# Retention and balanced experts as one stage: where the routing work stands between two layers of a language-model tower

## The reference, cut to what matters

```python
# retention: 8 heads of 16, causal with decay, group norm, gate, output projection
scores = jnp.einsum('bhtd,bhsd->bhts', q, k) / jnp.sqrt(jnp.float32(dh))
out = jnp.einsum('bhts,bhsd->bhtd', scores * decay[None], v)
return jax.nn.silu(x @ W_G + _group_norm(out)) @ W_O
# balanced experts: 8 experts, each sequence by itself
t = jnp.log(jnp.clip(einsum(x, gate_weight), 1e-6))
for _ in range(8):                                  # Sinkhorn
    t = t - logsumexp(t, axis=-2, keepdims=True)    # over the 512 tokens
    t = t - logsumexp(t, axis=-1, keepdims=True)    # over the 8 experts
vals, idx = top_k(exp(t) transposed, 512 // 8)      # 64 tokens for each expert
out[idx] = vals * (x[idx] @ experts[e])             # a later expert overwrites
```

## Time and profile before

| | |
|---|---|
| median of 3 runs | 2459.11 us (2454.38 to 2466.83) |
| the profiled execution's own time | 2457.47 us |
| its span | 2455.7 us |
| busy in the span: PE, DVE, ACT, POOL | 78%, 74%, 56%, 12% |

### The profile page before, as it was taken

One profiled execution on the slowest core, in us unless ns is written; L12 is line 12 of the kernel. 1 busy time (PEld: TensorE's weight loads), 2 busy tenths in 40 slices (PEclk: granted clock), 3 DMA queues, 4 the chain that ended last, 5 costly groups with the idle time before them and its releaser, 6 DMA issues. The chain is left out here.

```text
span 2455.7 us, 33355 instructions
## 1 busy us (share of the span) xinstructions
PE 1925.8 (78%) x11810; PEld 955.2 (39%) x11810; DVE 1805.2 (74%) x5024; ACT 1383.4 (56%) x1659; POOL 285.7 (12%) x332
## 2 busy tenths in 40 slices
PE   4999995886385699999999999999999776524933
PEld 2566654665131133333333333333334432313822
DVE  2676565665698899999999999999997677641513
ACT  0232221221056999999999999999998211101400
POOL 5000111001001000000000000000000000174373
PEclk8889996885597999999999999999999888656966
DMA  6300000001000100000000000000000000314521
GB/s 191 127 1 35 1 1 20 1 1 52 0 26 29 61 1 1 1 1 1 1 1 1 1 1 1 1 1 1 1 1 1 7 0 0 147 44 126 153 68 51
DMA packets 50149, 71.20 MB, mean 29 GB/s; under 512 B 8000, under 2 KB 36176, under 8 KB 49232
## 3 DMA queue, kind: packets, MB, share of 16 engines
q1 hardware_dynamic: 41264, 46.15, 5.5%
q0 software_dynamic: 8736, 23.10, 3.2%
HBM read 39.87 MB, written 23.07 MB: 26 GB/s over the span
## 5 line engine op out<-in xcount | busy, mean ns | idle before, releaser
L1751 ACT ACTIVATE KM<-KM 128x2048 f32<-128x2048 f32 x311 | 595.5, 1936 | 3.6 <-DVE KM L1601 3.6
L1601 DVE TENSOR_SCALAR KM<-big 128x512 f32<-128x512 f32 x1244 | 513.9, 480 | 24.1 <-PE bank L1878 16.7
L1878 PE MATMUL bank<-KM,w_a_wa 128*32 128x512 f32 x2736 | 370.5, 615 | 77.3 <-ACT KM L1751 60.5
L1751 ACT ACTIVATE aa_args<-aa_args 128x2048 f32<-128x2048 f32 x153 | 294.5, 1937 | 1.5 <-DVE aa_args L1601 1.5
L184 POOL TENSOR_TENSOR nrstd<-nrstd,minus_half 128x4 f32<-128x4 f32 (+1 forms) x82 | 84.2, 1047 | 1766.2 <-DVE nrstd L161 1729.2
L1851 PE MATMUL bank<-rf_wgu,XT 128*128 128x512 f32 x512 | 280.8, 634 | 1.2 <-DVE t512b L1660 1.2
L1601 DVE TENSOR_SCALAR aa_args<-big 128x512 f32<-128x512 f32 x612 | 253.9, 481 | 6.2 <-PE bank L1878 5.9
L1878 PE MATMUL bank<-aa_args,w_a_wa 128*32 128x512 f32 x1360 | 182.7, 610 | 37.4 <-ACT aa_args L1751 28.2
L1878 PEld LDWEIGHTS bank<-KM,w_a_wa 128*32 128x32 f32 x2736 | 54.3, 108 | 287.5 <-ACT KM L1751 190.0
L1851 PEld LDWEIGHTS bank<-rf_wgu,XT 128*128 128x128 f32 x512 | 77.4, 188 | 178.0 <-issue 173.7
L1656 DVE SCALAR_TENSOR_TENSOR ST<-ST,bank 128x256 f32<-128x256 f32 x256 | 106.3, 415 | 43.9 <-ACT ST L1741 43.8
(11 more groups left out here) (387 smaller groups left out, 3279.4 us busy)
## 6 DMA issues: line engine op xcount, KB each, us to landing
queues<-zeros SPq DMA_DIRECT2D x1, 8192.0 KB, 24.8
KM<-queues SPq DMA_DIRECT2D x32, 256.0 KB, 2.9
results<-KM POOLq DMA_DIRECT2D x32, 256.0 KB, 2.8
w<-in_w SPq DMA_DIRECT2D x1, 4096.0 KB
big<-in_w_pairs SPq DMA_DIRECT2D x1, 4096.0 KB
mf_tv<-in_task_W SPq DMA_DIRECT2D x1, 2048.0 KB, 10.2
la_v<-in_task_W SPq DMA_DIRECT2D x1, 2048.0 KB, 7.7
big<-XT SPq DMA_DIRECT2D x8, 256.0 KB, 2.3
```

The costliest lines, as they stand in the source:

```text
L1601: last = nc.vector.tensor_scalar(ARG(n, step)[:, cc, :], KU[:, i * T:(i + 1) * T], q, None, ALU.add)
L1751: last = nc.scalar.activation(ARG(n, step), ARG(n, step), ACT.Tanh)
L1878: last = nc.tensor.matmul(m.bank[g][32 * cc:32 * cc + 32, :], w["a_wa"][:, 30 - 2 * k:62 - 2 * k], ARG(n, step)[:, cc, :], start=k == 0, s ...
```

## The change

The two functions become one, `retention_and_balanced_experts`, without the barrier between them and with buffers of its own for the gates and the normalised input (`xta`, so no DMA puts it aside).

1. Gate front. The norm, transposes and gate matmuls of pair 0 stand inside retention's pair 1, those of pair 1 inside pair 2, those of pairs 2 and 3 around the end of pair 3. No loops; new transposes write the banks that retention's transposes use.
2. Sinkhorn in two halves of four sequences. Half 0 has one round after each of the eight score units of retention's pair 3, and its `max` rounds follow before the variances are read. Half 1 comes after retention, with two tiles of half 0's expert sum in each of its eight rounds. The selection is done once for each half, on 32 partitions instead of 64.
3. Expert sum. DVE takes experts 0 to 3 as four chained `scalar_tensor_tensor` into `h`, two tiles alternating. ACT weighs experts 4 to 7 as before, and POOL adds those in three steps (256, 128 and 128 elements per partition), the last into `h`. Matmul results have three pairs of banks.
4. The three weights of the experts are loaded with retention's.

```diff
@@ POOL
+            nc.gpsimd.memset(SEL, 0.0).then_inc(rest_zero.sem, 1)
...
+            for n in range(HALVES * TILES):
+                pool.wait_ge(scaled.sem, scaled.at(n, 1))
+                nc.gpsimd.tensor_tensor(y[:, 0:2, :], y[:, 0:2, :], y[:, 2:4, :], ALU.add).then_inc(four_sb.sem, 1)
+                pool.wait_ge(four_sb.sem, four_sb.at(n, 1))
+                nc.gpsimd.tensor_tensor(y[:, 0, :], y[:, 0, :], y[:, 1, :], ALU.add).then_inc(two_sb.sem, 1)
+                pool.wait_ge(two_sb.sem, two_sb.at(n, 1))
+                pool.wait_ge(acc[n % 2].sem, acc[n % 2].at(n // 2, 4))
+                nc.gpsimd.tensor_tensor(h, h, y[:, 0, :], ALU.add).then_inc(out_sb.sem, 1)
@@ DVE, in the loop over retention's pairs
-                masks(i)
                 if i + 1 < PAIRS:
+                    masks(i, range(len(UNITS)))
                     norm.vector(dve, i + 1, norm.pair(i + 1), XN)
+                    if i:
+                        gate_norm(i - 1)
+                else:
+                    for u in range(len(UNITS)):
+                        masks(i, (u,))
+                        for part in range(6):
+                            balance(0, u, part)
+                    for r in range(M // 8):
+                        ranked(0, r)
...
+                if 0 < i < PAIRS - 1:
+                    gate_logits(i - 1)
...
                 if i + 1 < PAIRS:
                     states(i + 1)
+                else:
+                    gate_norm(i - 1)
@@ DVE, behind it
+            selected(0)
+            gate_norm(PAIRS - 1)
+            gate_logits(PAIRS - 2)
+            weighted(0)
+            kept(0)
+            gate_logits(PAIRS - 1)
+            for k in range(ITERS):
+                for part in range(6):
+                    balance(1, k, part)
+                    if part < 4:
+                        summed(2 * k, part)
+                        summed(2 * k + 1, part)
+            for r in range(M // 8):
+                ranked(1, r)
+            selected(1)
+            weighted(1)
+            kept(1)
+            for n in range(TILES, 2 * TILES, 2):
+                for e in range(4):
+                    summed(n, e)
+                    summed(n + 1, e)
@@ PE, the expert matmuls
+            def expert(n):
+                if n >= 3:
+                    pe.wait_ge(acc[(n - 3) % 2].sem, acc[(n - 3) % 2].at((n - 3) // 2, 4))
+                    pe.wait_ge(scaled.sem, scaled.at(n - 3, 1))
+                for q in range(2):
+                    last = nc.tensor.matmul(m.bank[E_B(n)[q]][:, :], xta[:, b * T + c * P:b * T + (c + 1) * P], w["experts"][:, 512 * q:512 * q + 512],
+                                            start=True, stop=True)
@@ PE, the order
+                    for u in range(len(UNITS)):
+                        scores(i, (u,))
+                        columns(0, u)
+                    attend(i, (0,))
+                    turn_gates(0)
+                    attend(i, (1,))
                 variances(i)
+                if nxt and i:
+                    turn_b(i - 1)
+                if nxt:
                     keys(i + 1)
                 widen(i)
+                if nxt and i:
+                    logits(i - 1)
...
+            turn_b(PAIRS - 2)
+            logits(PAIRS - 2)
+            later(0)
+            turn_b(PAIRS - 1)
+            turn_weights(0)
+            logits(PAIRS - 1)
+            expert(0)
+            expert(1)
+            for k in range(ITERS):
+                columns(1, k)
+                for n in (2 * k + 2, 2 * k + 3):
+                    if n < TILES:
+                        expert(n)
+            turn_gates(1)
+            later(1)
+            turn_weights(1)
+            pe.wait_ge(w_sb.sem, 2)
+            for n in range(TILES, 2 * TILES):
+                expert(n)
```

More of the change, by code:

```diff
@@ L897, in _, with retention_and_balanced_experts @@
             down(3)
-def retention(ctx, nc, m):
+def retention_and_balanced_experts(ctx, nc, m):
     S = range(2)
@@ L971, in states, with masks @@
                         nc.vector.tensor_tensor(ST[s][:, c * P:(c + 1) * P], TB[s][:, 0:P], w["same_head"][:, :], ALU.mult).then_inc(st_sb.sem, 1)
-            def masks(i):
-                for u, (s, half, pair) in enumerate(UNITS):
+            def masks(i, us):
+                for u in us:
+                    s, half, pair = UNITS[u]
                     dve.wait_ge(sc_ps.sem, sc_ps.at(i, u + 1))
@@ L1045, in values, with turned_b, scale @@
                     nc.scalar.copy(V[s][:, :, :], v).then_inc(v_sb.sem, 1)
+            def turned_b(i):
+                for s in S:
+                    act.wait_ge(xb_ps.sem, xb_ps.at(i, s + 1))
+                    nc.scalar.copy(xta[:, (2 * i + s) * T:(2 * i + s + 1) * T], TB[s][:, :]).then_inc(xb_sb.sem, 1)
+            def scale(n):
+                act.wait_ge(e_ps.sem, e_ps.at(n, 1))
+                if n >= 4:
+                    act.wait_ge(out_sb.sem, out_sb.at(n - 4, 1))
+                for e in range(4):
+                    last = nc.scalar.activation(YW[n % 4][:, e, :], m.bank[E_B(n)[1]][:, e * D:(e + 1) * D], ACT.Copy, scale=weight(n, 4 + e))
+                last.then_inc(scaled.sem, 1)
             act.wait_ge(wv_ps.sem, 1)
@@ L1068, in _ @@
                     values(i + 1)
+            turned_b(PAIRS - 2)
+            turned_b(PAIRS - 1)
+            for h in range(HALVES):
+                act.wait_ge(w_sb.sem, w_sb.at(h, 1))
+                for n in range(h * TILES, (h + 1) * TILES):
+                    scale(n)
         @block.tensor
@@ new lines, in logits, with columns @@
+            def logits(i):
+                if i == 0:
+                    pe.wait_ge(m.loaded["gate_w"], 16)
+                for s in S:
+                    pe.wait_ge(xb_sb.sem, xb_sb.at(i, s + 1))
+                    for c in range(NC_):
+                        t = (2 * i + s) * T + c * P
+                        last = nc.tensor.matmul(TB[s][:, c * E:(c + 1) * E], xta[:, t:t + P], w["gate_w"][:, :], start=True, stop=True)
+                    last.then_inc(lg_ps.sem, 1)
+            def columns(h, k):
+                if k == 0:
+                    pe.wait_ge(lg_sb.sem, lg_sb.at(2 * h + 1, 2))
+                    pe.wait_ge(h_sb.sem, h_sb.at(2 + h, 2))
+                else:
+                    pe.wait_ge(sink_sb.sem, sink_sb.at(h * ITERS + k - 1, 6))
+                nc.tensor.matmul(OB[0][:, 0:NC_ * HE], w["ones"][:, 0:P], G8[h][:, :], start=True, stop=True).then_inc(col_ps.sem, 1)
@@ new lines, in turn_gates, with later @@
+            def turn_gates(h):
+                pe.wait_ge(sink_sb.sem, sink_sb.at(h * ITERS + ITERS - 1, 6))
+                for c in range(NC_):
+                    last = nc.tensor.transpose(GT_B(h)[0:HE, c * P:(c + 1) * P], G8[h][:, c * HE:(c + 1) * HE], w["ident"][:, :])
+                last.then_inc(gt_ps.sem, 1)
+            def later(h):
+                if h == 0:
+                    pe.wait_ge(m.loaded["later_expert"], 16)
+                    pe.wait_ge(rest_zero.sem, 1)
+                pe.wait_ge(sel_sb.sem, sel_sb.at(h, 1))
+                nc.tensor.matmul(LATER_B(h)[0:HE, :], w["later_expert"][:, 0:HE], SEL, start=True, stop=True).then_inc(later_ps.sem, 1)
@@ new lines, in turn_weights @@
+            def turn_weights(h):
+                pe.wait_ge(w_in.sem, w_in.at(h, 1))
+                for c in range(NC_):
+                    last = nc.tensor.transpose(W_B(h)[:, c * P:(c + 1) * P], SEL[:, c * P:(c + 1) * P], w["ident"][:, :])
+                last.then_inc(w_ps.sem, 1)
+            def expert(n):
+                b, c = at_tile(n)
+                if n == 0:
+                    pe.wait_ge(m.loaded["experts"], 16)
+                    pe.wait_ge(w_sb.sem, 1)
+                if n == 2:
+                    pe.wait_ge(lg_sb.sem, lg_sb.at(PAIRS - 1, 2))
+                if n >= 3:
[4 more added lines that the diff above has]
+                                            start=True, stop=True)
+                last.then_inc(e_ps.sem, 1)
```

366 lines of the change are left out of this document (143 added, 223 removed).

## The result

| | before | changed |
|---|---|---|
| median of 15 runs each | 2459.11 us (2452.63 to 2471.04) | 2445.77 us (2439.82 to 2452.25) |
| ratio, 95% interval | | 0.9936 (0.9921 to 0.9951) |
| profiled execution, its span | 2457.47, 2455.7 us | 2440.76, 2438.5 us |
| the stage, from layer 0's last addition to layer 2's first statistics | 387.66 to 741.01 = 353.35 us | 392.90 to 723.35 = 330.45 us |

Windows of the changed kernel (columns as in the earlier trace rows): pair 1, the masks of pair 3 with the rounds of half 0, the second Sinkhorn, the last 16 tiles.

A forecast was written before the change was run, and what follows sets the result against it. PE was taken as nearly full in retention's pairs, Sinkhorn and selection as one-engine chains with the others idle. Terms 10.8 + 14.3 + 7.6 + 2.9 - 12.0 + 10.7 - 32.6 = +1.7 us gave 2461 us, range 2449 to 2475.

The forecast's parts named there:

- seven terms with a sign: Steps of the stage: +10.8, +14.3, +7.6, +2.9, -12.0, +10.7, -32.6 us; an eighth, selection of half 1, was 0.
- The second Sinkhorn: Half 1's rounds with half 0's expert sum: 5.8 us a round, 1.6 of it idle, 44.8 against 34.1: +10.7 us.
- The expert sum: The last 16 tiles after selection: 2.1 us a tile, 39.2 in all against 71.8: -32.6 us.
- PE's ring: Expert sum: PE may write tile n + 3 only after tile n is summed, stalling about 0.5 us a pair.
- Pairs 1 and 2: Retention pairs that each gain a norm, 8 transposes and 8 gate matmuls: 5.4 us each, +10.8 us.
- Masks with rounds: Pair 3's masks with half 0's Sinkhorn: a unit of 3.4 us, eight units 27.2 against 12.9: +14.3 us.
- From the last addition to the second Sinkhorn: From retention's last addition to half 1's first column sum: 22.7 us against 34.7: -12.0 us.
- (a): Rival: POOL bounds the expert sum; at 2.9 us a tile the sum is +14.5, 2474 us; chance 0.18.
- (b): Rival: PE's clock stays low in the second Sinkhorn, price +12 us, 2473 us; chance 0.08.
- (c): Rival: inserted work costs the pairs nothing, last part 1.75 us a tile, 2444 us; 0.17 with what lies beyond.
- The port: DVE and POOL disturbing each other in SBUF: 0.13 us an instruction, 2 us over the rounds, some 5 by the skill's rule.

The follow-up runs named there:

- the repeat: The changed kernel with no edit, profiled a second time on another chip: 0.9943 against the kernel before.
- the other profile of before: The kernel before with no edit, profiled a second time, one execution: stage 354.2 us, pairs 1 and 2 together 83.1 us.
- all three edits together: Changed kernel with staggered rounds, a fourth pair of banks for the last 16 tiles, and transposes behind the keys: 0.9870 against the kernel before.
- the staggered rounds: Changed kernel, second Sinkhorn only: one expert tile ahead of PE's column sum instead of two, DVE's second tile two steps later: 0.9891 against the kernel before.

## Why the prediction was wrong

The recorded forecast was no change, 2461 us in 2449 to 2475. It came out at 2445.8, below the range. The waits stand where they were put, but for two short ones, and each of the seven terms with a sign has the one it was given. The sizes were off: in seven of the eight in the first profile, in six in the repeat, the cost was put too high or the gain too low. The step that failed is the cost of short DVE instructions, above all in the second Sinkhorn's round.

*The second Sinkhorn* failed most: +10.7 was +3.9. The wait was right (1.6 against 1.55). The work was not: "a round on DVE is 1.8 plus eight multiply-adds of 0.306", 4.2, is 3.40. Eight multiply-adds in a row take 2.16, 0.27 each; the mean of the earlier trace rows was that of other, shorter bursts. And between a round's steps they cost less than in a row. The bare round takes 1.94, its mixed one adds to it only 3.40 - 1.94 = 1.46 for multiply-adds that take 2.16 in a row. In the bare round the reciprocal starts 0.33 after the column sum that it needs; in the mixed one a multiply-add starts 0.21 after it. The 0.12 between them is time in which a dependent step waits, and independent work uses it. Seven periods that are 0.84 shorter and a last round that is 0.8 shorter make the 6.7. By the Trainium skill (VectorE: DVE Perf Modes, The DRAIN you can't avoid) the next instruction does not start until the pipe is empty, but one that is not held starts earlier. These rows do not show which instructions are held; they show both starts, 0.33 and 0.21, behind the same reduction of 0.29.

*The expert sum*: 39.2 to its end was said, and at least 1.2 more to layer 2's first statistics as before; 36.6 and 37.8 came. POOL was put at 2.1 a tile and takes 1.75 where it waits for nothing (0.80 + 0.53 + 0.42 from start to start). The line through 1.36 and 0.21 gave 0.50 for 128 elements where the row shows 0.45, and "0.1 for each dependent step" is 0.08 and less. With POOL out of the way PE's ring decides, as the prediction's stall of 0.5 a pair had it, at 3.72 - 3.43 = 0.29. The first result came after 3.29 instead of 4.2 in the first profile, but after 3.94 in the repeat, so most of that saving was not the kernel's.

*Pairs 1 and 2*: +10.8 was +8.0, or +5.6 against the other profile of before. The prediction's "period of 42.0 us" is the length of its window; mask to mask the two pairs took 41.1 and 39.6, and now 43.9 and 44.8, where "near 47" was said. In pair 1 the keys start 6.0 behind the end of the first norm (486.33 - 480.32) where it was 3.7, so 2.3 later and not 3.0, and the gate matmuls take 1.7 (493.94 to the values' first at 495.64): 4.0 a pair, 8.0 for two. Pair 1 alone grew by only 2.8, because its `widen` had run at the low clock before (16 matmuls in 3.62 us) and did not now (2.05). The 0.5 by which DVE's moved multiply was to delay the rest did not appear.

*Masks with rounds*: a unit is 3.05, not 3.4: masks 1.20, the round 1.85, and no wait at all for the column sum.

*From the last addition to the second Sinkhorn*: -12.0 was -13.4 and -15.9. The 22.7 was put together mostly at the low clock, and part of the stretch ran at the full one, by a part that changes from run to run (22.2 and 22.7 in the kernels with four pairs of banks and with the transposes behind the keys, whose code here is the same).

*Rivals.* (a), POOL as the bound at 2.9 a tile, fell: POOL itself waits 0.30 in every pair of tiles, and a pair falls to 3.43 with more banks. (b), the low clock in the rounds, fell: the granted clock is 1.00 there. (c) gave 2444, near the time, and that is luck: it had no cost in the pairs, which paid 8.0, and a last part 2.9 too short (1.75 a tile, where it is 1.86); the second Sinkhorn (6.8) and the masks (2.7), of which it said nothing, made up for both.

*The port.* The prediction read 0.13 of disturbance from a mean of 464 ns in the earlier trace rows. That mean hides two kinds. The shortest, median and longest of the same 16 instructions in ns, then one of the longest with POOL's addition beside it:

```profile
L431 DVE TENSOR_SCALAR XN<-h,mf_mean,mf_rstd x16: 333/335/1374, 289.4 to 345.5; 128x128 f32<-128x128 f32 x16
...
291.11 1.40 POOL L300 TENSOR_TENSOR h<-h,mf_ln 128x512 f32<-128x512 f32 x1
...
291.22 1.37 DVE L431 TENSOR_SCALAR XN<-h,mf_mean,mf_rstd 128x128 f32<-128x128 f32 x1
```

The last of eight scalings takes 1.37 and ends 0.1 after POOL's addition of 1.40; most others are not touched. Two of 1.37 among fourteen of 0.335 make the mean of 464. In the changed kernel's rounds the multiplies took 0.28 to 0.30, but they hardly meet POOL there: the first stands in its idle time, the second begins as an addition ends. Where they do meet, in the first round of all three edits together, DVE's multiply takes 0.83 instead of 0.29:

```profile
623.49 0.73 POOL L991 TENSOR_TENSOR KM<-KM 128x256 f32<-128x256 f32 x1 [12.38 <-ACT KM L1223]
...
623.53 0.83 DVE L1052 TENSOR_TENSOR be_gates<-be_gates,be_colsum 128x128 f32<-128x128 f32 x1
```

In the staggered rounds POOL is the one that loses, 0.77 to 0.87 for an addition of 0.73, and DVE's L1051 takes 0.33. By the Trainium skill's rule (SBUF — State Buffer, Who interferes with whom) one of the two waits out the other's whole instruction; the rows with 1.37 and 0.83 agree. The 2 us that the prediction allowed were not needed, since the instructions rarely fell together, and no step of the sum hung on it.

*The sum as a whole.* Each duration had been read whole and each hand-over added to it, in terms of 8 to 40 short instructions, so the errors lean one way and add: 2.8 + 2.7 + 6.8 + 2.7 are 15 of the 16 us between forecast and the repeated profile. The range was built from rivals and left this out.

*The clock in the pairs.* Pairs of the same code differ by up to 2.5 us, and their length goes with PE's granted clock, mask to mask:

| | granted clock | length |
|---|---|---|
| pairs without a front | 0.87 | 39.6 (once 40.3) |
| | 0.83 | 41.1 |
| | 0.78 to 0.80 | 42.0 to 42.1 |
| pairs 1 and 2 with a front | 0.88 | 43.9 |
| | 0.85 | 44.8 |

At the highest clock a front costs 43.9 - 39.6 = 4.3, and one row lower 44.8 - 41.1 = 3.7, so the +8.0 is the fair reading and the +5.6 had the slower pairs to compare with. What stays open is why the clock falls in one pair and not in the next; no run controlled it.

## What to carry to other kernels

Cost short instructions by the pitch of a burst (start to start), not by their duration, and count a dependent step's latency as free room for independent work between two steps. When two chains share an in-order queue, ask first in which order the shared engine meets their instructions: one tile's shift on PE, with DVE's order to match, was worth 7 us here, more than the whole new sum by itself (5.7), and moving work to another engine was worth nothing while a wait stood there anyway. A new sum's gain may lie in what it no longer waits for (4.0 of 5.7 us came with the DMAs), so test that part alone. And look at the longest instruction of a group before you use its mean.

## What the hardware showed unexpectedly

- Chained `scalar_tensor_tensor` of 128 x 128 from PSUM: 0.35 alone, 0.51 to 0.60 for two, 2.16 for eight of two chains alternating.
- POOL adds 128 x 128 float32 in 0.45 and 128 x 256 in 0.72 us, against 0.49 for two of DVE's 128 x 128. Beside it most of DVE's instructions lose nothing, and single ones as much as the rest of POOL's instruction: 1.37 for 0.335, 0.83 for 0.29.
- The clock's change of level moves the stretch between last addition and second Sinkhorn, the same code, from 18.8 to 22.7 us between runs.
- POOL, given the additions, and DVE, keeping them, end at the same time: a round of 4.96 and a pair of tiles of 3.72 in both, the pair for two different reasons.
